# Down stage by pairs of tiles: seven block products in place of eight

## The reference

```python
# x: 64 sequences x 32 rows x 512; per sequence an adapter number and a condition number
def lora_add(base, inp, A, B):                       # rank 16, one of 16 adapters per sequence
    t = einsum('bri,bni->bnr', A[index], inp)
    return base + einsum('bor,bnr->bno', B[index], t) * 0.5
gate = lora_add(x @ W_gate.T, x, A_gate, B_gate)      # 512 -> 1376
up   = lora_add(x @ W_up.T,   x, A_up,   B_up)
act  = silu(gate) * up
down = lora_add(act @ W_down.T, act, A_down, B_down)  # 1376 -> 512
h    = x + down
out  = h + einsum('bct,bcd->bdt', h, weights[condition])   # mixes the 32 rows of a sequence
```

## Time and profile before

| | us |
|---|---|
| median of 3 runs (448.95 to 449.59) | 449.36 |
| the profiled execution | 446.79 |
| its span, first to last instruction | 445.0 |
| TensorE busy, of the span | 438.1 |
| VectorE busy | 335.2 |
| ScalarE busy | 212.3 |

### The profile page before, as it was taken

The page is one execution under the profiler, slowest core; times in us unless marked ns, Lnnn a source line. Parts: engine busy times, 40 slices in busy tenths (PEclk is TensorE's granted clock), DMA queues, the critical chain, the costliest instruction groups (busy, mean ns, idle before and its releaser), DMA issues.

```text
span 445.0 us, 7248 instructions
## 1 busy us (share of the span) xinstructions
PE 438.1 (98%) x2475; PEld 393.5 (88%) x2475; DVE 335.2 (75%) x623; ACT 212.3 (48%) x397; POOL 169.7 (38%) x156
## 2 busy tenths in 40 slices
PE   8989999999999999999999999999999999999997
PEld 6877888888888888888888888999999999999996
DVE  6779999878867867857857858978667767766665
ACT  6746355366444544543543444843454454444531
POOL 2722223121121221121121452675776666756620
PEclk9999999999999999999999999999999999999999
DMA  8975664356555665665565599947776665556631
GB/s 243 381 242 146 181 172 114 109 172 188 145 181 151 159 172 145 161 173 144 159 173 144 145 287 340 247 138 202 215 201 208 208 180 178 177 178 196 191 96 47
DMA packets 99843, 81.12 MB, mean 182 GB/s; under 512 B 50944, under 2 KB 83200, under 8 KB 99808
## 3 DMA queue, kind: packets, MB, share of 16 engines
q1 hardware_dynamic: 88512, 47.27, 37.9%
q0 software_dynamic: 11008, 33.30, 24.8%
q10 hardware_dynamic: 288, 0.10, 0.1%
HBM read 65.18 MB, written 15.47 MB: 181 GB/s over the span
## 4 chain that ended last, share of the span: by engine, by line
PE 92%; DMA 2%; POOL 2%; issue 2%; DVE 1%; ACT 1%; SPq 0%; POOLq 0%
PE bank L1384 28%; PE bank L1262 9%; PE bank L1263 9%; PE bank L1261 9%; PE bank L1216 7%; PE bank L1217 7%; PE bank L1218 7%; PE bank L1283 4%; PE bank L1284 4%; PE bank L1414 2%; POOL a_raw L453 2%; PE bank L1394 2%; DMA b_raw<-in_b_rows,rows 2%; DMA gu_landing<-in_w_gate 1%; PE bank L1399 1%
## 5 line engine op out<-in xcount | busy, mean ns | idle before, releaser
L453 POOL DMA_INDIRECT b_raw<-in_b_rows,rows x48 | 51.8, 1078 | 188.7 <-DVE b_gu L803 188.1
L1384 PE MATMUL bank<-wd,actT_hi 128*128 128x288 f32 (+1 forms) x636 | 109.9, 295 | 0.0
L1384 PEld LDWEIGHTS bank<-wd,actT_hi 128*128 128x128 f32 (+1 forms) x636 | 93.8, 188 | 1.4 <-issue 0.2
L453 POOL DMA_INDIRECT a_dn_raw<-in_a_dn_rows,rows x64 | 77.3, 1208 | 19.5 <-issue 19.5
L803 DVE SCALAR_TENSOR_TENSOR b_gu<-b_raw,low_rows,b_gu 128x1024 fp32r<-128x1024 f32 (+1 forms) x48 | 55.6, 1159 | 26.8 <-ACT b_gu L513 26.8
L1384 PE MATMUL bank<-wd,actT_lo 128*128 128x288 f32 (+1 forms) x318 | 68.1, 296 | 0.0
L513 ACT ACTIVATE b_gu<-b_raw 128x1024 fp32r<-128x1024 f32 (+1 forms) x48 | 46.2, 963 | 11.2 <-DMA b_raw<-in_b_rows,rows 9.8
L1384 PEld LDWEIGHTS bank<-wd,actT_lo 128*128 128x128 f32 (+1 forms) x318 | 51.0, 188 | 0.0
L603 ACT ACTIVATE act<-bank 128x512 f32<-128x512 f32 (+1 forms) x48 | 26.1, 546 | 41.4 <-PE bank L1284 41.4
L910 DVE TENSOR_TENSOR act<-act,bank 128x512 f32<-128x512 f32 (+1 forms) x48 | 29.8, 621 | 8.6 <-PE bank L1284 7.8
L799 DVE TENSOR_TENSOR actT_lo<-actT_raw,actT_hi 128x1280 fp32r<-128x1280 f32 (+1 forms) x32 | 27.0, 886 | 11.6 <-ACT actT_hi L513 11.6
(11 more groups left out here) (180 smaller groups left out, 1004.2 us busy)
## 6 DMA issues: line engine op xcount, KB each, us to landing
actT_raw<-actT_dram SPq DMA_DIRECT2D x16, 640.0 KB
actT_dram<-staging SPq DMA_DIRECT2D x64, 128.0 KB, 2.9
x_sb<-in_x SPq DMA_DIRECT2D x16, 256.0 KB, 2.9
xT_raw<-in_xT SPq DMA_DIRECT2D x15, 256.0 KB, 2.7
out<-out_sb SPq DMA_DIRECT2D x15, 256.0 KB
a_raw<-in_a_gu_rows SPq DMA_DIRECT2D x56, 64.0 KB, 2.7
actT_dram<-staging SPq DMA_DIRECT2D x32, 88.0 KB, 3.2
wd_raw<-in_w_down SPq DMA_DIRECT2D x10, 256.0 KB, 5.9
```

The source lines that it names most:

```text
L453: return pool.indirect_dma_start(dst, None, src, bass.IndirectOffsetOnAxis(ap=rows[:, tile, col:col + 1], axis=0))
L1384: last = pe.matmul(ps_down[e][half][:, 0:HALF], a[e][0:n, c, :], wd[0:n, c, part, at:at + HALF], start=(c == 0 and i == 0), stop=(c == NC ...
```

## The change

For tiles 4 to 13, two tiles (m even and m+1) are worked as one product of 2 x 2 blocks: two tiles by two halves of the first 1280 rows of W_down (5 chunks each) by two halves of its 512 columns. By Winograd's scheme that takes seven block products instead of eight. It needs four sums of activation blocks (s1 to s4, on VectorE, each 128x640, written over `actT_raw0` and `actT_raw1`, but for s1), four sums of W_down's blocks (once), their splits, and adds and copies between PSUM banks. The last chunk (96 rows) stays plain. A block product is 15 matmuls of 256 columns, or of 320 where the adapter's 64 columns ride along. Tiles 0 to 3, 14 and 15 stay plain, with halves of 320 and 256 columns.

Besides, B_down is split once for all adapters into a table in DRAM, and the mix likewise, with the identity added to it (`b_table`, `mix_table`, three rounds in gate/up pairs 3 to 5; each round is one pass of ScalarE and one or two of VectorE over 512 columns). GpSimd then gathers split rows of B_down; SyncE loads a tile's mix in four small transfers. `residual_out` becomes a copy from PSUM on ScalarE (`copy_out`), since the mix now holds the identity.

```diff
+HC = (NC - 1) // 2
+LEFT, RIGHT = slice(0, RR + HALF), slice(RR, 2 * RR + HALF)
+FIRST_HALF, SECOND_HALF = slice(RR, RR + HALF), slice(2 * RR + HALF, WD)
...
             def load_actT(m, e):
                 for s in range(NS):
                     sp.wait_ge(spilled[s], 64 * (m // 2 + 1) if isinstance(m, int) else 64 * PAIRS)
+                if e == 0 and m > PLAIN_DN:
+                    sp.wait_ge(s24_ready, dn(m - 2))
                 reached(sp, actT_ready, m - 1)
-                reached(sp, down_done, m - 2)
...
+            for m in range(PLAIN_DN, LAST_DN, 2):
+                load_actT(m + 3, 1)
+                load_actT(m + 2, 0)
+                for e in range(2):
+                    store(m - 2 + e, e)
+                    load_x(m + e, e)
+                    load_mix(m + e, e)
...
+            def split_even(m):
+                sc.wait_ge(actT_landed[0], 32 * (m // 2 + 1))
+                if m == PLAIN_DN:
+                    sc.wait_ge(down_done, m - 1)
+                else:
+                    sc.wait_ge(dn_p2_done, dn(m - 2))
+                hi(actT_hi[0][:, 0:NC - 1, :], actT_raw[0][:, 0:(NC - 1) * P].rearrange("p (c n) -> p c n", n=P))\
+                    .then_inc(e_hi_ready, 1)
...
+            def copy_dn_p1(m):
+                sc.wait_ge(dn_p1_done, dn(m))
+                reached(sc, h_summed, 2 * (m - 2) + 2)
+                if m == PLAIN_DN:
+                    sc.wait_ge(zeros_set, 1)
+                hi(x3_[:, HALF:HALF + RR], zeros[:, :])
+                hi(x3_[:, 0:HALF], x0_[:, RR:RR + HALF]).then_inc(dn_p1_copied, 1)
+            def copy_dn_p7(m):
+                sc.wait_ge(dn_p7_done, dn(m))
+                reached(sc, dn_u7_ready, dn(m) - 1)
+                hi(e_dn[:, :], x2_[:, 0:HALF]).then_inc(dn_p7_copied, 1)
...
+            def copy_out(m, e):
+                sc.wait_ge(mix_done, 2 * (m + 1))
+                reached(sc, stored[e], 16 * (m // 2))
+                hi(out_sb[e][:, :], ps_mix[e][:, 0:H]).then_inc(out_ready, 1)
...
+            def seven_down(m):
+                further = m + 2 < LAST_DN
+                copy_dn_p1(m)
+                if m == PLAIN_DN:
+                    split_td(3)
+                    split_h(3, 1)
+                    split_a_dn(PLAIN_DN + 1, 1)
+                    split_odd(PLAIN_DN + 1)
+                copy_dn_p7(m)
+                if m > PLAIN_DN:
+                    copy_out(m - 2, 0)
+                if further:
+                    split_even(m + 2)
+                split_td(m)
+                copy_dn_t(m)
+                copy_out(m - 1, 1)
+                if further:
+                    split_s3(m + 2)
+                    split_s1(m + 2)
+                split_a_dn(m + 2, 0)
+                if further:
+                    split_even_last(m + 2)
+                else:
+                    split_actT(m + 2, 0)
+                split_td(m + 1)
+                split_h(m, 0)
+                split_h(m + 1, 1)
+                split_a_dn(m + 3, 1)
+                if further:
+                    split_odd(m + 3)
+                    split_s24(m + 2)
+                else:
+                    split_actT(m + 3, 1)
...
+            a11, a12 = actT_raw[0][:, 0:HC * P], actT_raw[0][:, HC * P:2 * HC * P]
+            a21, a22 = actT_raw[1][:, 0:HC * P], actT_raw[1][:, HC * P:2 * HC * P]
+            def sum_s1(m):
+                ve.wait_ge(actT_landed[1], 32 * ((m + 1) // 2 + 1))
+                nc.vector.tensor_tensor(s1_raw[:, :], a21, a22, ALU.add).then_inc(s_summed, 1)
+            def sum_s3(m):
+                ve.wait_ge(actT_landed[0], 32 * (m // 2 + 1))
+                ve.wait_ge(s_summed, 4 * dn(m) - 3)
+                nc.vector.tensor_tensor(a21, a11, a21, ALU.subtract).then_inc(s_summed, 1)
+            def sum_s2(m):
+                ve.wait_ge(s_summed, 4 * dn(m) - 2)
+                nc.vector.tensor_tensor(a11, s1_raw[:, :], a11, ALU.subtract).then_inc(s_summed, 1)
+            def sum_s4(m):
+                ve.wait_ge(s_summed, 4 * dn(m) - 1)
+                nc.vector.tensor_tensor(a12, a12, a11, ALU.subtract).then_inc(s_summed, 1)
...
+            def add_u3(m):
+                ve.wait_ge(dn_p7_copied, dn(m))
+                ve.wait_ge(dn_p6_done, dn(m))
+                nc.vector.tensor_tensor(x4_[:, 0:HALF], x3_[:, 0:HALF], e_dn[:, :], ALU.add).then_inc(dn_u3_ready, 1)
+            def add_u7(m):
+                ve.wait_ge(dn_t_copied, dn(m))
+                nc.vector.tensor_tensor(x2_[:, 0:HALF], x3_[:, 0:HALF], e_dn[:, :], ALU.add).then_inc(dn_u7_ready, 1)
...
+            def seven_down(m):
+                further = m + 2 < LAST_DN
+                split_s24(m)
+                if m == PLAIN_DN:
+                    mask_td(3, 1)
+                    residual_h(3, 1)
+                    split_a_dn(PLAIN_DN + 1, 1)
+                    split_odd(PLAIN_DN + 1)
+                add_u3(m)
+                if further:
+                    split_even(m + 2)
+                mask_td(m, 0)
+                if further:
+                    sum_s1(m + 2)
+                    sum_s3(m + 2)
+                add_u7(m)
+                if further:
+                    sum_s2(m + 2)
+                    sum_s4(m + 2)
+                    split_s3(m + 2)
+                    split_s1(m + 2)
+                split_a_dn(m + 2, 0)
+                if further:
+                    sum_a_dn(m + 3)
+                    split_even_last(m + 2)
+                else:
+                    split_actT(m + 2, 0)
+                mask_td(m + 1, 1)
+                residual_h(m, 0)
+                residual_h(m + 1, 1)
+                split_a_dn(m + 3, 1)
+                if further:
+                    split_odd(m + 3)
+                else:
+                    split_actT(m + 3, 1)
...
+            def dn_product(out_, a, c0, weights, cols, first=False):
+                for c in range(HC):
+                    for i, (at, part) in enumerate(((0, 0), (0, 1), (1, 0))):
+                        last = pe.matmul(out_, a[at][:, c0 + c, :], weights(c, part)[:, cols],
+                                         start=(first and c == 0 and i == 0), stop=(c == HC - 1 and i == 2),
+                                         skip_group_check=True)
+                return last
...
+                dn_product(x0_[:, wide], even, 0, b1, LEFT, True).then_inc(dn_p1_done, 1)
+                if m == PLAIN_DN:
+                    down_lora(3, 1)
+                pe.wait_ge(h_summed, 2 * (m - 1) + 2)
+                pe.wait_ge(s3_ready, dn(m))
+                pe.wait_ge(td_ready, 1)
+                dn_product(x2_[:, half], s31, 0, t13, T_SECOND, True).then_inc(dn_p7_done, 1)
+                pe.wait_ge(dn_p1_copied, dn(m))
+                dn_product(x0_[:, wide], even, HC, b2, LEFT).then_inc(dn_p2_done, 1)
+                pe.wait_ge(s24_ready, dn(m))
+                pe.wait_ge(td_ready, 2)
+                dn_product(x3_[:, half], s24, 0, t42, T_SECOND).then_inc(dn_p6_done, 1)
+                last_chunk(x0_[:, wide], 0, LEFT).then_inc(down_done, 1)
+                if m > PLAIN_DN:
+                    mix(m - 2)
+                pe.wait_ge(dn_u3_ready, dn(m))
+                pe.wait_ge(s1_ready, dn(m))
+                pe.wait_ge(a_dn_ready, m + 2)
+                dn_product(x3_[:, wide], s31, HC, t13, with_a).then_inc(dn_p5_done, 1)
+                mix(m - 1)
+                pe.wait_ge(actT_ready, m + 2)
+                pe.wait_ge(dn_t_copied, dn(m))
+                dn_product(x4_[:, wide], odd, HC, t42, with_a)
+                pe.wait_ge(dn_u7_ready, dn(m))
+                last_chunk(x3_[:, half], 0, SECOND_HALF).then_inc(last_chunk_done[0], 1)
+                down_lora_half(m, 0, 0)
+                lora_products(m, 0, 1)
+                last_chunk(x4_[:, wide], 1, RIGHT).then_inc(down_done, 1)
+                dn_product(x3_[:, half], s24, HC, b2, SECOND_HALF).then_inc(down_lora_done, 1)
+                last_chunk(x2_[:, half], 1, SECOND_HALF).then_inc(last_chunk_done[1], 1)
+                down_lora(m + 1, 1)
```

657 lines of the change are left out of this document (442 added, 215 removed).

## The result

The changed kernel takes 505.52 us (median of 4, 503.74 to 507.87), the kernel before 449.46 beside it (448.95 to 449.59): 1.1253 times as long, 95% interval 1.1206 to 1.1300. I had forecast 481 in a range of 466 to 496. Slower was right, the size was not: the last matmuls start at 502.69 us where I had 473.2.

What follows compares the result with a forecast made beforehand. TensorE bound the kernel before; afterwards a ring of VectorE's list, load and split (17.7 + 5.3 + 1.3 = 24.3 us a pair) plus the way in put the last matmuls 31.7 us later: 449.36 to 481, range 466 to 496.

Steps and rivals of the forecast that it cites:

- TensorE's and VectorE's sums: Down stage, per pair of tiles: TensorE's matmuls 18.16 us against 19.84 before, VectorE's list of work 17.7 us.
- The list: VectorE's fixed work per pair, from the even tile's low part to that of s2 and s4: 17.7 us.
- The ring: Steady pairs: VectorE's list, then the even tile's load after `s24_ready` (5.3) and high-part split (1.3): 24.3 us a turn.
- the second way round: From `s24_ready` over ScalarE's first-product copy, later products, mix and output copy to the even tile's split: 5.1 us.
- ScalarE copies the first product only after its pass over s2 and s4 ... the copy about 1.0 ahead of it: Step in each pair: ScalarE's copy follows that pass, about 1.0 us ahead of `s24_ready`, and releases the second product.
- The start of the kernel ... stay: Before the Down stage: start unchanged, the stage beginning within 1 us of 282; the kernel's end stays too.
- The way in: First Down tiles up to the first pair: VectorE's 20.8 us put its `s24_ready` at 333.7; first turn 30.5.
- one gather less: GpSimd has one gather less; with the mix's small transfers this costs nothing, 0 to 1 us.
- By the row, none: Clock: judging by the trace at 25 to 30 us, no stretch would run at 1.2 GHz.
- The rival of 506: The clock falls in TensorE's gaps: second way round about 10 us, 481 + 25 = 506; chance 0.07.
- The gap filled: Rival: load and first-product copy are hidden, turns 18.5 to 20, only the way in costs: 460; chance 0.09.
- TensorE the bound: Rival: TensorE stays the bound in the pairs, 8.4 us gained, 441; chance 0.06.

Runs made afterwards that it cites:

- e11: Changed kernel with one A_down gather instead of four for each tile from 6 on, output incomplete: 491.09 us, 1.0901 of the kernel before.
- e12: Changed kernel with gathered mix, own s2/s4 buffer, early first-product copy, early even tile, A_down of tiles 6 to 15 by SyncE transfers: 483.83 us (1.0756).
- e2: Changed kernel with ScalarE's copy of the first product moved ahead of its pass over s2 and s4: 488.08 us, 1.0901 of the kernel before.
- set 1: First four edited kernels beside the kernel before, without the changed kernel itself: 490.46, 488.08, 487.85 and 488.56 us against 448.06.
- b1: The kernel before, unaltered, run again for its trace: 449.45 us.
- e1: Changed kernel with fixed mix rows, so without SyncE's register work for the mix, output incomplete: 490.46 us, 1.0959 of the kernel before.
- e8: The same kernel as e1, run again beside the unaltered changed kernel: 499.76 us, 1.1128 of the kernel before.
- e13: Changed kernel with own s2/s4 buffer, early first-product copy, early even tile, and an odd tile's gathers put behind P6: 484.42 us (1.0807).
- sets 1 and 3: Set 3 ran the unaltered changed kernel, fixed mix rows and two gathered-mix kernels: 509.36, 499.76, 515.48 and 492.18 us, before 448.66; for the other see set 1.

## Why the prediction was right and wrong

**TensorE's and VectorE's sums: right.** P1's fifteen matmuls of 320 columns take 2.21 us, 0.147 each, and those of 256 columns come every 0.119. The list took 17.6 us against 17.7. Neither product count nor passes were mis-sized.

**The ring: right in mechanism and, by itself, in size.** Turns of 24.5 to 25.0 (e11) against 24.3; with an own buffer and the even tile early they are 20.5 to 21.0 (e12). In e2 and e11 the load takes 6.1 from `s24_ready`, where I took 5.3 between 4.55 and 7.45; the second way round takes 4.9 in e11 where I had 5.1. Where no signal in the pairs is over 1.3 us late, with VectorE's list and the ring as in the change, the times are 487 to 494 (set 1) and 491 (e11), inside the range of 466 to 496.

**"ScalarE copies the first product only after its pass over s2 and s4 ... the copy about 1.0 ahead of it": this step failed.** It took a signal as given when the matmul ends, as in every row I had, so the copy would follow the pass. In the changed kernel the copy waits for a signal held in GpSimd's burst: 2.5 us behind the pass in pair 8, 3.9 in pair 10, 5.5 in pair 12, and behind it hang P2, P6, the mix, the copy of the output and the even tile. In pair 6 the copy was where I had it, and the signals of P7, P2 and P6 were held instead: VectorE waits 6.7 us for the add of u3, until 380.82. The turns were 26.8, 27.8 and 30.2 instead of three times 24.3 (+11.9), and the end 43.8 instead of 36.1 (+7.7), of which 5.4 because the last pair's P2 starts 4.5 us after `s24_ready` instead of 0.9 before. I had looked at GpSimd only for "one gather less". The change made more than that: b_dn waits for the pair's adapter and both tiles' A_down for the splits at the pair's end, so the gathers of two tiles became one group of ten, and it runs exactly while P1 and P7 finish. The bursts are what the runs show in this step's place; what turns a burst into a late signal stays open (below).

**"The start of the kernel ... stay": wrong by 3.5 us.** The Down stage starts at 285.79, not within 1 us of 282. TensorE waits for nobody from 40 to 284, before and after, but its matmuls of 512 columns between 110 and 250 come every 232 ns where they came every 227 (medians). e2 and e12 have the same 232, b1 has 227, so it goes with the changed program and not with the set. Why is open; I had the first stage's edits at nothing.

**The way in: too short.** `s24_ready` of the first pair comes at 341.6, not 333.7 (+7.9), the first turn is 32.5, not 30.5 (+2.0). Of the 7.9, 3.5 is that late start and 2.8 a late signal of tile 1 (VectorE waits 2.82 us for `down_done` at 311.2, as gathers run to 310.5). Without late signals (e2) it was +3.2, all of it the late start (285.63), and +3.2 in the first turn, which ran at the half clock for 14 us there and 7 here; no run tells what that cost. The four parts, 7.9, 2.0, 11.9 and 7.7, are the 29.5 us by which the last matmul starts later than forecast.

**"By the row, none": wrong on the clock.** From tile 4 to the last pair the granted clock is at half for 31 us in all: three times in the first pair, never in the second, once in each of the others. The full clock at 25 to 30 was no measure, since the longest gap there was 1.5 us; here it falls with each of TensorE's five gaps of 3.5 to 6.9 us, and once behind one of 1.9. P2 of tile 8 takes 3.6 us instead of 2.2. The rule of the Trainium skill ("TensorE: Matmul & The Clock Gate", section "Part 1: The HAM clock gate") is that idleness brings the low clock back. The trace agrees for those five gaps; behind nine more of 1.1 to 2.0 us the clock stayed at full.

**The rival of 506 had the right number and the wrong mechanism.** Pairs of 27 us and more with a clock below 1.00 were to be its sign, and both were there; that its number fits is luck. e2 has 34 us at the low clock, a mean of 0.965 against 0.969, and is 17 us faster. e1 and e8, the same kernel, say it more plainly: 38 us at the low clock and 490.96 us in e1's trace, 17 us and 495.32 in e8's, where signals are held. The clock is a consequence of the gaps and costs some us; it is not what makes the 24. What told them apart was a run with as much low clock and no late signals.

**The gap filled, or TensorE the bound:** no run got there. The best (e12, e13) are 8% above the kernel before, with turns over 19.84 (from 20.5 in e12, from 22.7 in e13) and a start of tile 4 24 and 15 us late.

**Open.** What holds the signals. They need GpSimd's bursts (e11), but in set 1 the same ten gathers ran (387.85 to 400.5 in e2) and P1's signal at 391.3 was on time. The chip does not decide it either: sets 1 and 3 ran on the same one. What goes with held signals in every trace is an incomplete record of the semaphores' updates: 9114 to 9130 updates in set 1 (none held), 6018 to 7093 in the other traces of changed kernels; 8165 in the first trace of the kernel before (none held), 5411 in b1. All executions here were recorded, so none tells whether an unrecorded one would have held signals at all; this is the rival that I left untested. The Trainium skill ("Perfetto Trace Analysis", section "Per-engine timelines") says that TensorE's end in a trace is estimated and its signal is pushed when PSUM has acknowledged the writes, so an end in a row is no proof of a signal; that fits 396.63 against 401.73. The Trainium skill ("NOTIFIC — the notification-queue block", section "7.1 Overflow: three behaviours, one of which stalls the engine") also says that the path of such records can hold its producers back; the counts fit that, and no run here shows it. I also did not try to move u3 behind the even tile's low part on VectorE.

## What to carry to other kernels

A wait ends with a signal, not with the last row of work: where a profile names a remote or unknown releaser, compare the semaphore's own update with the matmul's end before you blame an order or a clock. When a change makes dependencies coarser (a pair in place of a tile), ask for every queue, GpSimd's too, how its work now bunches and what it will run beside. And keep the changed kernel itself in each set of runs: set 1 alone would have given two edits the credit for what neither did in a later set.
